# A tile table built in three parts, weights copied inside the last attention unit, and a routing exponential placed ahead of the first tile's silu

## The chip, the cores and the metric

One core of a Trainium2 chip runs the whole program. The metric is the device time of one execution in microseconds. The kernel before was timed three times: median 1210.19 us, from 1207.68 to 1212.79. One further execution was profiled; every row shown of the kernel before comes from it.

The engines are called PE (TensorE, with its weight loads apart as PEld), DVE (VectorE), ACT (ScalarE), POOL (GpSimd) and SP (SyncE, which here only issues transfers). Each runs its own list of instructions in order and waits at semaphores for the others.

## The reference

The input is 16 sequences of 512 tokens with 128 features. Two layers follow, each with a residual sum and a layer norm.

```
x = layernorm(x + attention(x))
x = layernorm(x + experts(x))
```

Attention has 16 heads of 8 features. Its softmax is taken twice over: half of the result is the usual softmax, half is the softmax without key 0, normalised again.

The expert layer routes every token to two of eight experts. The logits are x times gate_w; top 1 and top 2 are chosen, and each gets as its weight the softmax over those logits that lie within a jitter threshold of it:

```
mask1 = (m1 - logits) / maximum(abs(logits), m1) > 0.02
p1    = softmax(where(mask1, -inf, logits))     # weight of the first choice
mask2, p2 likewise for the second choice, the first one dropped
out  += wte[:, e] * ((silu(x @ w1[e].T) * (x @ w3[e].T)) @ w2[e].T)
```

All of this is computed in fp32 results, though scores are formed from bf16 parts.

## The kernel before

**Attention.** The work is cut into 64 units: a sequence (b, 0 to 15) and a group of four heads (g, 0 to 3). A loop over periods p runs on every engine, with eight steps k in each. In period p, PE forms the score products of unit p (two per step, 16 in all), ACT turns each into an exponential, and PE multiplies the exponentials of unit p - 1 with the values (four groups of eight matmuls, at the odd steps), which gather in one PSUM bank, acc_ps. DVE frees that bank by transposing it (`sums_by_query`), at step 0 of the period after. Score products pass through a ring of three PSUM banks, so PE can be at most three ahead of ACT. The row maxima of a unit are formed two periods ahead, so in the last two periods (62 and 63) there are none.

**Beside it.** While sequence b is attended to, the older ones are finished: normalised sums, output projection, layer norm (`ln_stats`, `ln_moments` on DVE, `inverse_deviation` on POOL, which also forms the logits), and the routing, 20 small DVE operations (`route(b, step)`) placed by the table ROUTE. Routing needs two results of ACT: `magnitudes` (absolute logits) and `routing_exp`, the exponential of the distances, which waits for the first eight steps. POOL's indirect transfers then scatter each token's row, twice, into the regions of its experts in rows_d.

**The tile table.** Rows of one expert are taken 256 at a time, as tiles. FIRST = 45 tiles are certain once 13 sequences are counted. `first_tables` on DVE, placed in period 62 at step 2, works out for each of them its expert, the first row in rows_d and the offset of its weights. It is a chain of small operations, each of which waits for the one before. Its parts are `whole_tiles`, `running_sum`, `tile_places` (expert of each tile, and the step within it), `tile_rows` (which ends with the semaphore s_tab_done) and `take` (how many tiles of each expert are used up).

**The expert tiles.** For each tile t, SP loads the rows by blocks (`load_blocks`, waits for s_tab_done) and once more whole (`load_rows`); DVE turns the blocks (`turn_rows`); ACT copies the expert's quarter of W1 and W3 out of the resident weights (`copy_weights`, two copies of 128x512, offsets read from the table); PE does `tile_up` (eight matmuls, L712), `tile_down` of the tile before (16 matmuls, L738), `tile_lin` (eight, L722); ACT the silu; DVE the product of both and the weighted result; POOL scatters the result into y_d. `tail(t)` on DVE and POOL, and a few lines on ACT, finish the last two sequences beside the first tiles. PE's values of the last unit (63) stand at t = 0 around the first tile, two groups ahead of `tile_lin(0)` and two behind. A last stage adds both results of each token to form the second layer norm.

**At the seam.** The order is written out by hand. Before its first tile, PE waits for the table, for all exponentials of the ring (s_ring_done, TAIL) and for all maxima. ACT waits, behind its last exponential, for the table, for W1 and W3, and copies the weights of tile 0, then of tile 1. DVE's list reads: the table (762 to 771 us), three routing steps of sequence 13, `sums_by_query(61)`, one more routing step, statistics, the turn of tile 0, `sums_by_query(62)`, nine routing steps of sequence 14. SP's list has, ahead of tile 4's blocks, the last quarter of W2 (`load_weights`, L470), which may go out once PE's last score product is done, since it overwrites keys and queries of attention. `tile_down(0)` waits for all of W2 (`pe.wait_ge(s_w2, 16 * NG)`).

Of the kernel before, what the change touches and what calls it, by code (L numbers as in the profile page):

```python
# [26 lines left out]
NB, L, D = 16, 512, 128  # L27
# [30 lines left out]
def layer(nc, xT, x, wqT, wkT, wvT, woT, bq, bk, bv, bo, gateT, w1T, w3T, w2T, out):  # L58
# [16 lines left out]
    with ctx:  # L75
# [501 lines left out]
        def _(pe):  # L577
# [146 lines left out]
                last.then_inc(s_lin, 1)  # L724

            def tile_down(t):
                if t == FIRST:
                    pe.wait_ge(s_tab_done, 3)
                expert = pe.value_load(woff_i[0:1, t:t + 1], min_val=0, max_val=(E - 1) * F)
                if t == 0:  # L730
                    pe.wait_ge(s_w2, 16 * NG)
                pe.wait_ge(s_h, t + 1)
                if t >= 2:
                    pe.wait_ge(s_y, t - 1)
                for w in range(halves(t)):
                    at = TK * (t % 2) + D * w
                    for c in range(FC):
                        last = nc.tensor.matmul(y_ps[:, at:at + D], HH[t % 2][:, c, P * w:P * (w + 1)],  # L738
                                                W2[:, bass.ds(expert + c * D, D)], start=(c == 0), stop=(c == FC - 1))
                last.then_inc(s_y_ready, 1)  # L740
# [5 lines left out]
                if (t, place) in TAIL_RING:  # L746
                    behind(*TAIL_RING[t, place])

            pe.wait_ge(s_tab_done, 1)
            pe.wait_ge(s_ring_done, TAIL)  # L750
            pe.wait_ge(s_mx_done, QC * UNITS)
            for t in range(TILES + 1):
                if is_tile(t):
# [24 lines left out]
        def _(act):  # L778
# [84 lines left out]
            def normed_rows(b, c):  # L863

                if c == 0:
                    act.wait_ge(s_rstd, 4 * (b + 1))
                nc.scalar.activation(XE[b % 2][:, c, 0, 0:D], ysum[:, c, :], ACT.Identity, scale=rstd[:, c:c + 1],
                                     bias=shift[:, c:c + 1]).then_inc(s_sent_step, 1)

            for p in PERIODS:  # L870
                b, g = divmod(p, NG)
                for k in range(STEPS):
                    if is_unit(p):
                        exp_chunk(p, 2 * k)
                        exp_chunk(p, 2 * k + 1)
                    if k == 1 and is_unit(p + 1):
                        negmax_rows(p + 1)
                    if (p, k) in ONCE:
                        behind(*ONCE[p, k])
                        if ONCE[p, k] == ("gw", 0):  # L880
                            for u in (0, 1):
                                load_first_queries(u)
                    if (g, k) in BEHIND:
                        name, off = BEHIND[g, k]
                        if is_seq(b + off):
                            behind(name, b + off)
                            if (name, b + off) == ("v1", 0):
                                for u in (2, 3):
                                    load_first_queries(u)
                    if g == 0 and k % 2 == 1 and is_seq(b - 2):  # L890
                        normed_rows(b - 2, k // 2)
                    if (g, k) == (0, 2) and is_seq(b - 2):
                        magnitudes(b - 2)
                    if (g, k) == (0, 6) and is_seq(b - 2):
                        routing_exp(b - 2)


            def copy_weights(t):
                if t >= 2:
                    act.wait_ge(s_lin, t - 1)  # L900
                if t == FIRST:
                    act.wait_ge(s_tab_done, 3)
                expert = act.value_load(woff_i[0:1, t:t + 1], min_val=0, max_val=(E - 1) * F)
                for to, held in ((W1T, W1), (W3T, W3)):

                    nc.scalar.activation(to[t % 2], held[:, bass.ds(expert, F)], ACT.Copy, scale=2.0)\  # L906
                      .then_inc(s_w_copied, 1)

            def small_tile_in(t):
                act.wait_ge(s_xgt_ready, t - FULL + 1)  # L910
# [1 line left out]
                nc.scalar.activation(XGT[t % 2][:, 0:n], xgt_ps[:, TK * (t % 2):TK * (t % 2) + n], ACT.Copy)\  # L912
                  .then_inc(s_xgt, 1)

            act.wait_ge(s_tab_done, 1)
            act.wait_ge(s_w13, 16 * 2 * NG)
            act.wait_ge(*split_done(NB - 1, 1))
            copy_weights(0)
            for t in range(TILES):
                if is_tile(t + 1):  # L920
                    copy_weights(t + 1)
                act.wait_ge(s_up, t + 1)
                if t == 0:
                    act.wait_ge(s_pv_ready, UNITS - 1)
                n = P * halves(t)
                nc.scalar.activation(SG[t % 2][:, :, 0:n], up_ps[:, :, 0:n], ACT.Silu).then_inc(s_silu, 1)  # L926
                if FULL <= t + 1 < TILES:
                    small_tile_in(t + 1)
                if t in (0, 10):
                    magnitudes(NB - 2 if t == 0 else NB - 1)  # L930
                if t in (2, 16):
                    for c in range(QC):
                        normed_rows(NB - 2 if t == 2 else NB - 1, c)
                if t in (1, 13):
                    routing_exp(NB - 2 if t == 1 else NB - 1)
                for place in range(2):
                    if (t, place) in TAIL_RING:
                        behind(*TAIL_RING[t, place])
# [12 lines left out]
        def _(dve):  # L951
# [180 lines left out]
            def tile_places(first, last):  # L1132
# [1 line left out]

                ge, gn = tile_by_expert(first, last)
                which = slice(first, last)
                no = tile_step[:, 0:last - first]

                def by_tile(x):
                    return x.unsqueeze(1).to_broadcast([1, last - first, E])  # L1140
# [4 lines left out]
                tb(V.tensor_tensor(ge, tile_no[:, 0:last - first].unsqueeze(2).to_broadcast([1, last - first, E]),  # L1145
                                   by_tile(cum), ALU.is_ge))
                tb(V.tensor_reduce(expert[:, which], ge, axis=AXX, op=ALU.add))
                tb(V.tensor_tensor(gn, ge, by_tile(move), ALU.mult))
                tb(V.tensor_reduce(no, gn, axis=AXX, op=ALU.add))

            def tile_rows(first, last, rows):
# [17 lines left out]
            def first_tables():  # L1169
# [7 lines left out]
                whole_tiles(cnt, TK)  # L1177
                running_sum()
                tile_places(0, FIRST)
                tile_rows(0, FIRST, TK)  # L1180
                take(FIRST)

            def full_by_expert():
                tb(V.tensor_tensor(cnt, offs[0:1, QC, :], eoff[0:1, :], ALU.subtract))
# [5 lines left out]
            def rest_by_expert():  # L1190
                tb(V.tensor_scalar_add(cnt, cnt, float(P - 1)))
                whole_tiles(cnt, P)
                tb(V.tensor_scalar(start, taken, float(HALVES), None, ALU.mult))
                tb(V.tensor_tensor(tiles, tiles, start, ALU.subtract))
                running_sum()

            for p in PERIODS:
                b, g = divmod(p, NG)
                for k in range(STEPS):
# [4 lines left out]
                    if is_seq(b - 1):  # L1204
# [8 lines left out]
                            ln_moments(b - 1, range(0, 1))  # L1213
                        elif (g, k) == (3, 4):
                            ln_moments(b - 1, range(1, 4))
                    if is_seq(b - 2) and (g, k) in ROUTE:
                        for step in ROUTE[g, k]:
                            route(b - 2, step)
                    if (g, k) == (3, 0) and is_seq(b - 1):
                        ln_stats(b - 1, range(0, 2))  # L1220
                    if (p, k) == (UNITS - 2, 2):
                        first_tables()


            def tail(t):
                if t == 0:
                    sums_by_query(UNITS - 2)
                    for step in range(0, 9):
                        route(NB - 2, step)
                elif t == 1:  # L1230
                    sums_by_query(UNITS - 1)
                    second_sums(NB - 1)
# [22 lines left out]
                    full_by_expert()  # L1255
                elif t == 24:
                    tile_places(FIRST, FULL)
                elif t == 26:
                    tile_rows(FIRST, FULL, TK)
                elif t == 28:  # L1260
                    take(FULL - FIRST)
                elif t == 30:
                    rest_by_expert()
                elif t == 32:
                    tile_places(FULL, TILES)
                elif t == 34:
                    tile_rows(FULL, TILES, P)

# [410 lines left out]
```

## Time and profile before

| | us |
|---|---|
| median of three runs | 1210.19 |
| profiled execution | 1210.04 |
| its span in the profile | 1208.3 |
| PE busy | 1129.0 (93%) |
| DVE busy | 918.8 (76%) |
| ACT busy | 831.2 (69%) |
| POOL busy | 660.6 (55%) |

Shares of busy time are means over three stages with different limits: attention (to about 786 us), tiles (to about 1160) and the last sums. The chain of waits gives PE 47% of the span and DVE 39%, of which the row maxima (L993) have 30%: they set the pace of attention, PE that of the tiles. The granted clock of PE has two levels here, 1.00 (2.4 GHz) and 0.50 (1.2 GHz); a value between them is a slice that holds both.

### The profile page before, as it was taken

Reading aid. Unit: us, or ns where it says so; the run is one execution under the profiler, and the core shown is the slowest. Engines: PE = TensorE matmul, PEld = TensorE weight load, DVE = VectorE, ACT = ScalarE, POOL = GpSimd, SP = SyncE. Lnnn points to the kernel's source line nnn. Section 1 sums busy time; section 2 is a strip of 40 time slices with the busy share of each in tenths; the row PEclk is TensorE's granted clock in tenths of the full one; section 3 lists DMA queues with packets and bytes.
Section 4 is the critical chain, followed back from the end, with each engine's and each line's share of the span. In section 5 each row is a group of like instructions: output and inputs, shape, how many; then the busy total and the mean of one; then the engine's idle time right before and its main releaser. Section 6 shows DMA issues by size and latency. Waiting matters only on the chain.

```text
span 1208.3 us, 23516 instructions
## 1 busy us (share of the span) xinstructions
PE 1129.0 (93%) x7114; PEld 564.7 (47%) x7117; DVE 918.8 (76%) x1328; ACT 831.2 (69%) x1691; POOL 660.6 (55%) x999
## 2 busy tenths in 40 slices
PE   4899999999999999999999998899999999999986
PEld 3322222222222222222222222169999999999952
DVE  6788999999999999999999999544545544443335
ACT  2278889889889889888888888654544443444636
POOL 4314546676676676676676654646545433333335
PEclk9889999999999999999999999789999999999999
DMA  5434344444444444444454454333434433321147
GB/s 163 138 94 123 104 117 129 119 132 127 121 133 126 122 131 125 121 135 122 123 135 115 123 148 150 90 75 80 93 74 103 90 78 74 79 64 40 42 162 265
DMA packets 170078, 138.46 MB, mean 115 GB/s; under 512 B 84564, under 2 KB 146648, under 8 KB 169953
## 3 DMA queue, kind: packets, MB, share of 16 engines
q1 hardware_dynamic: 160064, 117.22, 36.4%
q0 software_dynamic: 8688, 18.14, 4.5%
q10 hardware_dynamic: 1200, 1.57, 0.5%
q8 instruction: 60, 0.98, 0.4%
q14 instruction: 66, 0.53, 0.1%
HBM read 94.59 MB, written 42.19 MB: 113 GB/s over the span
## 4 chain that ended last, share of the span: by engine, by line
PE 47%; DVE 39%; issue 9%; DMA 2%; POOL 1%; ACTq 1%; SPq 1%; ACT 1%; POOLq 0%; DVEq 0%
DVE rowmax_sb L993 30%; PE ring_ps L738 10%; PE mx_ps L712 10%; PE mx_ps L722 10%; PE acc_ps L619 5%; PE ring_ps L607 5%; PE mx_ps L596 3%; DVE TN_sb L1002 3%; PE mx_ps L772 1%; PE ring_ps L652 1%; DVE stats_sb L1025 1%; DVE meanvar_sb L1032 1%; PE ring_ps L660 1%; DMA bo_sb<-bo 1%; DVE dist_sb L1060 0%
## 5 line engine op out<-in xcount | busy, mean ns | idle before, releaser
L794 ACT ACTIVATE probs_sb<-ring_ps 128x512 f32<-128x512 f32 x1024 | 558.2, 598 | 108.3 <-PE ring_ps L607 93.2
L993 DVE TENSOR_REDUCE rowmax_sb<-mx_ps 128x4 f32<-128x2048 f32 x256 | 585.8, 2288 | 32.3 <-PE mx_ps L596 26.8
L607 PE MATMUL ring_ps<-region_sb 74*128 74x512 bf16 x1024 | 315.9, 391 | 1.0 <-ACT probs_sb L794 0.9
L619 PE MATMUL acc_ps<-probs_sb,values_sb 128*32 128x512 f32 x2048 | 277.8, 616 | 4.1 <-DVE TN_sb L1002 4.1
L1628 POOL DMA_INDIRECT y_d<-probs_sb,values_sb x135 | 133.0, 985 | 206.4 <-DVE probs_sb L1293 182.3
L607 PEld LDWEIGHTS ring_ps<-region_sb 74*128 74x128 bf16 x1024 | 79.5, 97 | 321.3 <-ACT probs_sb L794 274.8
L906 ACT ACTIVATE xT_sb<-region_sb 128x512 f32 x78 | 49.1, 630 | 187.4 <-PE mx_ps L722 185.6
L1506 POOL DMA_INDIRECT rows_d<-sent_sb,pos_sb x128 | 130.2, 1017 | 41.0 <-issue 19.2
L1301 DVE TENSOR_TENSOR probs_sb<-mx_ps,probs_sb 128x1024 f32<-128x1024 f32 (+1 forms) x78 | 84.3, 1081 | 79.8 <-PE mx_ps L722 79.8
L596 PE MATMUL mx_ps<-k_maxima_sb,q_maxima_sb 32*128 32x512 bf16 x1024 | 101.9, 388 | 41.9 <-DVE rowmax_sb L993 41.5
L738 PE MATMUL ring_ps<-region_sb,probs_sb 128*128 x1080 | 135.8, 277 | 1.4 <-DVE probs_sb L1301 1.4
L1293 DVE SCALAR_TENSOR_TENSOR probs_sb<-ring_ps,values_sb 128x128 f32<-128x128 f32 x135 | 42.1, 347 | 121.1 <-issue 77.3
L712 PE MATMUL mx_ps<-k_parts_sb,xT_sb 128*128 128x256 f32 (+1 forms) x624 | 132.0, 355 | 1.9 <-ACT xT_sb L906 1.9
L738 PEld LDWEIGHTS ring_ps<-region_sb,probs_sb 128*128 128x128 f32 x1080 | 126.9, 191 | 12.5 <-issue 5.2
L712 PEld LDWEIGHTS mx_ps<-k_parts_sb,xT_sb 128*128 128x128 f32 x624 | 107.9, 192 | 15.2 <-issue 2.4
L619 PEld LDWEIGHTS acc_ps<-probs_sb,values_sb 128*32 128x32 f32 x2048 | 40.9, 109 | 103.9 <-issue 97.8
L596 PEld LDWEIGHTS mx_ps<-k_maxima_sb,q_maxima_sb 32*128 32x128 bf16 x1024 | 25.8, 91 | 115.0 <-DVE rowmax_sb L993 105.5
L926 ACT ACTIVATE probs_sb<-mx_ps 128x1024 f32<-128x1024 f32 (+1 forms) x78 | 70.5, 904 | 4.6 <-PE mx_ps L712 4.5
L722 PE MATMUL mx_ps<-k_parts_sb,full_q_sb 128*128 128x256 f32 (+1 forms) x312 | 65.6, 353 | 0.0
L722 PE MATMUL mx_ps<-k_parts_sb,full_k_sb 128*128 128x256 f32 (+1 forms) x312 | 64.6, 350 | 0.0
L1360 POOL CAST negmax_parts_sb<-negmax_sb 16x128 bf16<-16x128 f32 x64 | 17.9, 279 | 81.7 <-PE mx_ps L596 75.6
L722 PEld LDWEIGHTS mx_ps<-k_parts_sb,full_q_sb 128*128 128x128 f32 x312 | 51.6, 191 | 5.6 <-issue 1.1
(183 smaller groups left out, 1166.6 us busy)
## 6 DMA issues: line engine op xcount, KB each, us to landing
region_sb<-k_parts_d SPq DMA_DIRECT2D x64, 288.0 KB
region_sb<-q_parts_d SPq DMA_DIRECT2D x60, 288.0 KB
k_parts_d<-k_parts_sb SPq DMA_DIRECT2D x48, 256.0 KB, 2.5
k_maxima_sb<-k_parts_d SPq DMA_DIRECT2D x256, 32.0 KB
probs_sb<-y_d SPq DMA_DIRECT2D x32, 256.0 KB, 5.0
q_maxima_sb<-q_parts_d SPq DMA_DIRECT2D x244, 32.0 KB
values_sb<-rows_d SPq DMA_DIRECT2D x57, 132.0 KB, 2.2
q_parts_d<-q_parts_sb SPq DMA_DIRECT2D x16, 384.0 KB, 3.7
```

The costliest lines, as they stand in the source:

```text
L596: last = nc.tensor.matmul(mx_ps[:, j, :], q[rows, P * c:P * (c + 1)], k[rows, :], start=True, stop=True)
L607: nc.tensor.matmul(bank, KS[b % 2][0:KR + MR, h, P * c:P * (c + 1)], QS[b % 2][0:KR + MR, h, :], start=True, stop=True).then_inc(s_ring_re ...
L619: last = nc.tensor.matmul(acc_ps[VW * j:VW * (j + 1), 0, :], VE[b % 2][:, c, HG * g + j, :], PT[u % 2][:, j, c, :], start=(c == 0), stop=( ...
L712: last = nc.tensor.matmul(up_ps[:, c, 0:n], W1T[t % 2][:, P * c:P * (c + 1)], XGT[t % 2][:, 0:n], start=True, stop=True)
L722: last = nc.tensor.matmul(lin_ps[:, c, 0:n], W3T[t % 2][:, P * c:P * (c + 1)], XGT[t % 2][:, 0:n], start=True, stop=True)
L738: last = nc.tensor.matmul(y_ps[:, at:at + D], HH[t % 2][:, c, P * w:P * (w + 1)], W2[:, bass.ds(expert + c * D, D)], start=(c == 0), stop= ...
L794: nc.scalar.activation(PT[u % 2][:, i // QC, i % QC, :], ring_bank("st", u, i), ACT.Exp, scale=SCALE).then_inc(s_ring_done, 1)
L926: nc.scalar.activation(SG[t % 2][:, :, 0:n], up_ps[:, :, 0:n], ACT.Silu).then_inc(s_silu, 1)
L993: V.tensor_reduce(rowmax[u % 2][:, :].rearrange("p (j c) -> p j c", c=QC)[:, :, c], mx_ps[:, :, :], axis=AXX, op=ALU.max, negate=True).the ...
L1301: V.tensor_tensor(HH[t % 2][:, :, 0:n], lin_ps[:, :, 0:n], SG[t % 2][:, :, 0:n], ALU.mult)\
L1506: G.indirect_dma_start(rows_d, bass.IndirectOffsetOnAxis(ap=pos[b % 2][:, s, c:c + 1], axis=0), XE[b % 2][:, c, s, :], None).then_inc(s_sc ...
L1628: G.indirect_dma_start(y_d, bass.IndirectOffsetOnAxis(ap=XG[t % RING][:, w, D:D + 1].bitcast(i32), axis=0), YO[t % YRING][:, w, :], None, ...
```

## The change

DVE: `tile_places` loses its last two operations, which become `tile_steps`; `first_tables` ends after `tile_places`. `tile_steps` and `tile_rows` move to period 63, step 0, behind `sums_by_query(61)`. The routing steps 16 to 19 of sequence 13 (in periods 62, step 4, and 63, step 0) move to period 63, step 6, with `take` behind them. At the head of the tiles, routing steps 0 to 8 of sequence 14 change places with `sums_by_query(62)`.

ACT: the copies of tile 0's weights move, with their waits, into period 63 behind step 5, which is behind the twelfth of 16 exponentials. `magnitudes` and `routing_exp` of sequence 14 move from behind the silus of tiles 0 and 1 to ahead of the silu of tile 0.

PE: the waits for the table and for the ring's exponentials move from ahead of the first tile to the head of `tile_down(0)`.

```diff
@@ PE
             def tile_down(t):
+                if t == 0:
+                    pe.wait_ge(s_tab_done, 1)
+                    pe.wait_ge(s_ring_done, TAIL)
                 if t == FIRST:
...
-            pe.wait_ge(s_tab_done, 1)
-            pe.wait_ge(s_ring_done, TAIL)
             pe.wait_ge(s_mx_done, QC * UNITS)
@@ ACT (copy_weights itself is only defined earlier)
                     if (g, k) == (0, 6) and is_seq(b - 2):
                         routing_exp(b - 2)
+                    if (p, k) == (UNITS - 1, 5):
+                        act.wait_ge(s_tab_done, 1)
+                        act.wait_ge(s_w13, 16 * 2 * NG)
+                        act.wait_ge(*split_done(NB - 1, 1))
+                        copy_weights(0)
...
-            act.wait_ge(s_tab_done, 1)
-            act.wait_ge(s_w13, 16 * 2 * NG)
-            act.wait_ge(*split_done(NB - 1, 1))
-            copy_weights(0)
             for t in range(TILES):
                 if is_tile(t + 1):
                     copy_weights(t + 1)
+                if t == 0:
+                    magnitudes(NB - 2)
+                    routing_exp(NB - 2)
                 act.wait_ge(s_up, t + 1)
...
-                if t in (0, 10):
-                    magnitudes(NB - 2 if t == 0 else NB - 1)
+                if t == 10:
+                    magnitudes(NB - 1)
...
-                if t in (1, 13):
-                    routing_exp(NB - 2 if t == 1 else NB - 1)
+                if t == 13:
+                    routing_exp(NB - 1)
@@ DVE
                 tb(V.tensor_reduce(expert[:, which], ge, axis=AXX, op=ALU.add))
-                tb(V.tensor_tensor(gn, ge, by_tile(move), ALU.mult))
+
+            def tile_steps(first, last):
+                ge, gn = tile_by_expert(first, last)
+                no = tile_step[:, 0:last - first]
+                tb(V.tensor_tensor(gn, ge, move.unsqueeze(1).to_broadcast([1, last - first, E]), ALU.mult))
                 tb(V.tensor_reduce(no, gn, axis=AXX, op=ALU.add))
...
                 tile_places(0, FIRST)
-                tile_rows(0, FIRST, TK)
-                take(FIRST)
...
+            LAST_ROUTES = ((UNITS - 2, 4), (UNITS - 1, 0))
...
+                    if (p, k) == (UNITS - 1, 0):
+                        tile_steps(0, FIRST)
+                        tile_rows(0, FIRST, TK)
-                    if is_seq(b - 2) and (g, k) in ROUTE:
+                    if is_seq(b - 2) and (g, k) in ROUTE and (p, k) not in LAST_ROUTES:
                         for step in ROUTE[g, k]:
                             route(b - 2, step)
...
+                    if (p, k) == (UNITS - 1, 6):
+                        for at in LAST_ROUTES:
+                            for step in ROUTE[at[0] % NG, at[1]]:
+                                route(NB - 3, step)
+                        take(FIRST)
...
                 if t == 0:
-                    sums_by_query(UNITS - 2)
                     for step in range(0, 9):
                         route(NB - 2, step)
+                    sums_by_query(UNITS - 2)
```

The two later tables (at tiles 24 and 32) call `tile_steps` directly behind `tile_places`, so nothing changes there.

## Rows read from the trace of the kernel before

**Rows 1.** The page: granted clock of TensorE, in tenths, 40 slices of the span.
```profile
PEclk9889999999999999999999999789999999999999
```

**Rows 2.** Chain that ended last, at the seam: start us, us, what.
```profile
788.08 3.75 PE mx_ps L712 x8
...
794.83 1.93 PE mx_ps L722 x8
796.75 1.85 PE acc_ps L619 x16
798.60 1.93 PE mx_ps L712 x8
800.53 1.78 PE ring_ps L738 x16
```

**Rows 3.** Tiles: length, busy of PE PEld DVE ACT POOL, clock, DMA, GB/s.
```profile
900.00:1000.00 100.00, 100.00 (x611) 90.45 (x610) 51.28 (x129) 40.55 (x57) 45.47 (x47) 1.00 0.41 88
```

**Rows 4.** Timeline of PE: start, us, what, xcount, [idle before, releaser].
```profile
760.66 1.06 PE L619 MATMUL acc_ps<-probs_sb,values_sb 128*32 128x512 f32 x8
...
763.05 1.06 PE L619 MATMUL acc_ps<-probs_sb,values_sb 128*32 128x512 f32 x8
...
765.74 1.07 PE L619 MATMUL acc_ps<-probs_sb,values_sb 128*32 128x512 f32 x8
...
772.61 1.93 PE L619 MATMUL acc_ps<-probs_sb,values_sb 128*32 128x512 f32 x8 [4.12 <-DVE TN_sb L1002]
...
776.31 1.93 PE L619 MATMUL acc_ps<-probs_sb,values_sb 128*32 128x512 f32 x8
```

**Rows 5.** Stretches at the seam, columns as in rows 3.
```profile
770.00:771.00 1.00, 0.00 (x0) 0.00 (x0) 0.85 (x6) 0.00 (x0) 0.00 (x0) 0.61 0.26 74
794.00:796.00 2.00, 2.00 (x14) 1.12 (x7) 0.00 (x0) 0.00 (x0) 0.00 (x0) 0.97 0.33 70
```

**Rows 6.** Timeline of DVE at the seam, columns as in rows 4.
```profile
766.49 0.52 DVE L1147 TENSOR_REDUCE k_maxima_sb<-q_parts_sb 1x45 f32<-1x360 f32 x1
...
768.47 1.19 DVE L1155 TENSOR_TENSOR k_maxima_sb<-k_maxima_sb 1x45 f32<-1x45 f32 x1
...
770.55 0.17 DVE L1161 CAST k_maxima_sb<-k_maxima_sb 1x45 int32<-1x45 f32 x1
...
775.60 0.45 DVE L1275 STREAM_TRANSPOSE k_parts_sb<-q_maxima_sb 128x256 f32<-128x256 f32 x1 [1.16 <-DMA q_maxima_sb<-rows_d]
785.71 0.72 DVE L1002 STREAM_TRANSPOSE TN_sb<-acc_ps 128x512 f32<-128x512 f32 x1 [9.66 <-PE acc_ps L619]
...
786.75 1.98 DVE L1065 SCALAR_TENSOR_TENSOR absl_sb<-dist_sb,rev_sb 128x32 f32<-128x32 f32 x1
...
789.88 0.19 DVE L1065 SCALAR_TENSOR_TENSOR absl_sb<-dist_sb,rev_sb 128x32 f32<-128x32 f32 x1
```

**Rows 7.** Timeline of GpSimd (POOL) at the seam.
```profile
768.35 1.25 POOL L1451 TENSOR_TENSOR ysum_sb<-attn_out_sb,x_sb 128x512 f32<-128x512 f32 x1
774.52 0.20 POOL L1460 TENSOR_SCALAR rstd_sb<-meanvar_sb 128x4 f32<-128x4 f32 x1 [4.92 <-DVE meanvar_sb L1032]
...
787.39 1.28 POOL L1439 TENSOR_TENSOR x_sb<-x_sb,bo_sb 128x512 f32<-128x512 f32 x1
```

**Rows 8.** Timeline of ACT behind the last exponential.
```profile
786.22 0.60 ACT L794 ACTIVATE probs_sb<-ring_ps 128x512 f32<-128x512 f32 x1 [1.64 <-PE ring_ps L607]
787.30 0.63 ACT L906 ACTIVATE xT_sb<-region_sb 128x512 f32 x1 [0.49 <-issue]
...
789.51 1.28 ACT L926 ACT_TABLE_LOAD   x1
```

**Rows 9.** Timeline of SP; and landing of the weight load issued at 786.21.
```profile
783.85 0.40 SPq L530 DMA_DIRECT2D values_sb<-rows_d  x1
786.21 0.36 SPq L470 DMA_DIRECT2D region_sb<-w2T  x1
...
DMA to landing us min/median/max: 4.3/4.3/4.3
```

More of the change, by code:

```diff
@@ L868, in normed_rows, with copy_weights @@
                                      bias=shift[:, c:c + 1]).then_inc(s_sent_step, 1)
+            def copy_weights(t):
+                if t >= 2:
+                    act.wait_ge(s_lin, t - 1)
+                if t == FIRST:
+                    act.wait_ge(s_tab_done, 3)
+                expert = act.value_load(woff_i[0:1, t:t + 1], min_val=0, max_val=(E - 1) * F)
+                for to, held in ((W1T, W1), (W3T, W3)):
+                    nc.scalar.activation(to[t % 2], held[:, bass.ds(expert, F)], ACT.Copy, scale=2.0)\
+                      .then_inc(s_w_copied, 1)
             for p in PERIODS:
@@ L895, in _ @@
                         routing_exp(b - 2)
[L898 to L907, printed above, removed]
+                    if (p, k) == (UNITS - 1, 5):
[3 more added lines that the diff above has]
+                        copy_weights(0)
             def small_tile_in(t):
@@ L1136, in tile_places @@
                 which = slice(first, last)
-                no = tile_step[:, 0:last - first]
                 def by_tile(x):
@@ L1257, in tail @@
                     tile_places(FIRST, FULL)
+                    tile_steps(FIRST, FULL)
                 elif t == 26:
@@ L1265, in tail @@
                     tile_places(FULL, TILES)
+                    tile_steps(FULL, TILES)
                 elif t == 34:
```

## The prediction

> **What bounds the kernel now.** I read the page's clock line first: TensorE (PE) has its full clock in all but two places, and one slice near four fifths of the run stands at 7 [rows 1]. That slice is the seam between attention and the expert tiles. The chain of waits there goes through VectorE (DVE), PE, ScalarE (ACT) and PE again; from the first tile on it is PE alone, tile after tile [rows 2]. Table by stretch: PE is busy 100.00 of 100 us between 900 and 1000 [rows 3], 611 matmuls at 32 a tile, so 5.24 us a tile with no gap. What makes the first tile's down product start earlier therefore ends the run as much earlier, as long as transfers keep up.
>
> In the seam the timeline of PE shows the loss. The last attention unit but one runs at a pace of 763.05 - 760.66 = 2.39 us per pair of steps [rows 4]. Then PE idles 4.12 us (768.49 to 772.61) for the transposition that frees acc_ps, which stands on DVE behind the whole tile table. In this idle time the granted clock falls: 0.61 in the slice from 770 to 771 [rows 5], where PE had been idle since 768.49. Afterwards a pair takes 776.31 - 772.61 = 3.70 us [rows 4], and the first tile's up product 3.75 us where the same eight matmuls take 1.93 once the clock is back at about 794 [rows 2, 5].
>
> **The change part by part, on the profiled execution** (1210.04 us, its span 1208.3; the median of the runs shown is 1210.19, 0.15 above, which I neglect).
>
> *Table in three parts.* The first part now ends with the reduce of L1147, at 766.49 + 0.52 = 767.01 [rows 6]. The transposition of unit 61's sums follows at once, because its input was done at 765.74 + 1.07 = 766.81 [rows 4]. It takes 0.72 [rows 6], so the bank is free at about 767.8, before 768.49 when PE wants it. The 4.12 us go. If a DVE operation were held up as L1155 was (1.19 us instead of some 0.2), 0.4 us would come back; I take 0.
>
> *The table itself.* L1148 and L1149 come behind the transposition, some 0.7 us later than before; L1154 and L1155 then fall into GpSimd's residual sum of 1.25 us at 768.35 [rows 7], as L1155 did before (768.47 to 769.66). That held-up time swallows most of the 0.7: the table is ready at about 770.9 instead of 770.72 [rows 6]. SyncE (SP) starts its loads 0.2 us later; bounds 0 and 0.7. Nothing in unit 63's first half waits for the table any more.
>
> *Deferred routing of sequence 13 and "take".* They leave the place ahead of the moments and come behind them. GpSimd's deviation work was released by the moments at 774.52 [rows 7], 3.80 us after the table; without the take (four operations), three routing steps and the transposition in between it comes some 1.5 us earlier, and the four routing steps (under 1 us) run beside its first operations, ahead of the logits that wait for them. No cost; at worst 0.5 us on logits that have slack until the first tile's rows have landed and been turned at 775.60 + 0.45 [rows 6].
>
> *Unit 63.* At full clock its four groups of values start at about 768.5, 770.9, 773.3 and 775.7.
>
> *Weights copied behind the twelfth exponential.* Before, the copies came after the last exponential with a gap of 0.49, and four took 789.51 - 787.30 = 2.21 [rows 8], 0.55 each. Two cost ACT 0.49 + 1.10 = 1.6 us. PE meanwhile has one score product and the last values to do (1.06), so its last score product, which without copies would come at 775.7 + 1.06 = 776.7, waits for the thirteenth exponential: the twelfth ends at about 775.4, 1.6 for the copies and 0.60 more [rows 8] make 777.6, so 1.0 us is lost and the product starts at 777.7. Bounds: 0 if the three ring banks cover it all, 2.2 if nothing does. The table has been ready for 4 us by then, and SP issues the last loads of W1 and W3 in unit 60's period.
>
> *PE's waits moved into the first down product.* The first up product no longer waits for the last exponentials, only for turned rows (776.3) and copied weights (777.0): it starts at about 777.9 instead of 788.08. At full clock up, values, lin, values take 1.93 + 1.85 + 1.93 + 1.85 = 7.56 [rows 2], so up(1) starts at 785.5 and down(0) could start at 787.4, against 800.53: 13.1 us earlier.
>
> *Magnitudes and routing exponential ahead of the first silu; routing ahead of the transposition on DVE.* Behind the turn at 776.05 (+0.2) come nine routing steps. They took from 786.4, the end of the transposition, to 789.88 + 0.19 = 790.1, and one was held for 1.98 instead of some 0.2 [rows 6]; so 1.9 us without, 3.7 with: done at 778.2, or 780.0. Then the transposition of unit 62: 778.9 or 780.7. PE wants it after up(0), at 779.8, so it costs 0 to 0.9 us. On ACT: last exponential done at 777.6 + 3 x 0.60 = 779.4, two copies 1.6, magnitudes and exponential 0.5 (an estimate: the unheld routing steps of the same rows take 0.2 each on DVE), function load 1.28 [rows 8], silu 1.0 (an estimate: half of the 2.21 that four 128x512 copies took): done at 783.9, wanted by up(1) at 785.5. Hidden, with 1.6 us of cover; queued behind it on ACT are only later copies. Two later function loads go, beside a busy PE: nothing.
>
> *What is late next: the last quarter of W2.* SP's order is unchanged and it has no wait to lose: its row load for tile 1 was issued at 783.85 and ended at 784.25; only the weights behind it waited, until 786.21, for PE's last scores [rows 9]. These now come first, so the weights go out at about 784.5 and land 4.3 us later (what this transfer took), at 788.8. down(0) waits for them: 788.9 instead of 800.53. So of PE's 13.1 us, 1.5 us are given back, and the same 1.5 us hide small delays upstream (the DVE holding above, half of the uncertainty of the copies). Sum: 800.53 - 788.9 = 11.6 us earlier, 1210.04 - 11.6 = 1198.4 us. Later block and row loads come in the order and at the spacing of before, where PE never waited for them between 900 and 1000 [rows 3].
>
> **A rule against it.** In units 62 and 63 PE works through three ring banks with short idle times, and the trace keeps the full clock there until the long idle time begins [rows 4, 5]. The Trainium skill ("TensorE: Matmul & The Clock Gate", section "A second HAM failure mode: psum-queue depth-cycling") says that frequent micro-idles between matmul groups that cycle through PSUM banks can make the clock fall and rise again. No run here shows it for unit 63 without the 4.12 us; by that rule the first rival below would hold, by the row the forecast.
>
> **The rivals.**
> *The clock falls anyway,* at the 1.0 us for the copies or at the short waits around. For: the fall came 1.9 us into an idle time. Against: unit 62 held the clock. Price: if it falls at the copies, PE is fully busy from 777.9, and before, the clock came back at 794.3, 6.2 us after such work began at 788.08; 6.2 us at half clock lose 3.1, of which W2 hides 1.5: 1200.0. If it falls in the first half of unit 63, four pairs lose 1.3 each besides: 1205.2. Middle 1202.
> *The held-up DVE or the ACT order becomes the wait.* Two holdings of 1.75 us in the nine steps put the end of the transposition at 778.2 + 3.5 + 0.7 = 782.4, 2.6 after PE wants it: less the 1.5 that W2 hides, 1.1 us are lost, 1199.5; with first blocks landing 2 us later besides, 1201.5. For: GpSimd has eight scatters in this time. Against: the step held before ended with GpSimd's add of 1.28 us at 787.39 [rows 7], and that add now comes behind the scatters, after the nine steps.
> *It doesn't free PE:* the first part of the table still ends after 768.49 + 1.9, and the clock falls as before. Then the idle time is shorter by about 2 us and the copies overlap: 1205 to 1206. Against: the stretch up to L1147 is unchanged code with unchanged neighbours.
> *Slower:* the clock falls in unit 63 and the wait for W2 and for the first tiles' blocks breaks PE's work up again, so that it stays low into the tiles. Each tile at half clock costs 5.24 us more; from 11.6 / 5.24 = 2.2 tiles on the gain is gone, and with four tiles low the time is 1210.04 - 11.6 + 21.0 = 1219.4. Against: before, the clock rose before the second tile began, with worse gaps.
>
> **How the numbers follow.** Forecast 0.66 (1196.5 to 1200.5: W2 a little earlier or later, runs differing by some 2 us); clock falls 0.17 (1200 to 1205.2); DVE or ACT order 0.09 (1199.5 to 1201.5); PE not freed 0.05 (1205.5); slower 0.03 (1219.4). If W2 came without any wait the time would be 1196.9; a run 2 us low makes 1194.9. Range 1195 to 1204. About 0.5% (6 us, so below 1204.1 and above 1216.2) can be told from no change: faster 0.91, same 0.06, slower 0.03.
>
> **What would show it.** Right: in unit 63 no idle time of PE before L619, granted clock 1.00 through the seam, about 2.4 us a pair; two copies on ACT between exponentials; the first up product near 778, PE waiting 1 to 2 us in front of the first down product with W2's transfer as releaser; the first tile's silu before up(1); then tiles at 5.24 us. Wrong: half clock in any slice from 768 to 790, PE waiting for the transposition or ACT for the routing steps, or the first down product after 792.

## Result: 0.72% faster, by the seam as predicted, with a smaller gain in the medians than in the profile

| | us |
|---|---|
| before, median of 6 runs | 1208.76 (1206.94 to 1212.79) |
| changed, median of 6 runs | 1200.62 (1200.21 to 1201.15) |
| ratio, 95% interval | 0.9928 (0.9916 to 0.994) |
| predicted | 1198.4, range 1195 to 1204 |
| profiled execution changed | 1200.69, span 1199.0 |
| profiled execution before | 1210.04, span 1208.3 |

Three of the six runs of the kernel before are those whose median stands in its section on the time. The medians differ by 8.1 us, the two profiled executions by 9.35; the sum of the prediction was 11.6.

The page's clock line of the changed kernel has no 7 at the seam any more [rows 1]; the 8 at the right end lies behind the last product, the one near the left in the start, where nothing changed.

```profile
PEclk9989999999999999999999999999999999999998
```

The chain that ended last, changed kernel: it no longer comes from DVE's table through ACT's copies. It runs through SP's list of loads to the transfer of W2, and from there along PE [rows 2].

```profile
785.30 0.40 SPq L530
...
785.74 4.41 DMA region_sb<-w2T
...
790.28 2.05 PE ring_ps L741 x16
```

Timeline of PE, changed kernel (start, us, what, count, idle before and its releaser). The values of unit 62 follow without idle time at 2.4 us a group (769.43, 771.83, and so on to 776.62, where [rows 4] had 4.12 us of idle time and then 3.70 a group); the last score product waits 0.59 us for the copies; the first up product starts at 778.50 and takes 1.89, not 3.75. Then PE waits 2.33 us for W2.

```profile
766.74 1.07 PE L619 MATMUL acc_ps<-probs_sb,values_sb 128*32 128x512 f32 x8
...
769.43 1.07 PE L619 MATMUL acc_ps<-probs_sb,values_sb 128*32 128x512 f32 x8
...
771.83 1.07 PE L619 MATMUL acc_ps<-probs_sb,values_sb 128*32 128x512 f32 x8
...
776.62 1.06 PE L619 MATMUL acc_ps<-probs_sb,values_sb 128*32 128x512 f32 x8
778.28 0.39 PE L607 MATMUL ring_ps<-region_sb 74*128 74x512 bf16 x1 [0.59 <-ACT probs_sb L795]
778.50 1.89 PE L712 MATMUL mx_ps<-k_parts_sb,xT_sb 128*128 128x256 f32 x8
...
785.96 1.99 PE L712 MATMUL mx_ps<-k_parts_sb,xT_sb 128*128 128x256 f32 x8
790.28 2.05 PE L741 MATMUL ring_ps<-region_sb,probs_sb 128*128 x16 [2.33 <-DMA region_sb<-w2T]
```

The granted clock of four stretches over the seam, columns as in rows 3: 1.00 throughout, also over the 2.33 us of waiting (786 to 792), against [rows 5].

```profile
768.00:774.00 6.00, 5.48 (x32) 1.54 (x30) 5.15 (x20) 5.17 (x11) 1.64 (x3) 1.00 0.49 144
774.00:780.00 6.00, 5.15 (x29) 2.18 (x29) 3.61 (x19) 5.33 (x11) 4.67 (x9) 1.00 0.38 58
780.00:786.00 6.00, 6.00 (x43) 2.32 (x41) 1.99 (x4) 4.43 (x8) 4.47 (x6) 1.00 0.57 125
786.00:792.00 6.00, 3.67 (x27) 3.12 (x24) 3.01 (x7) 1.02 (x1) 2.14 (x2) 1.00 0.72 180
```

Timeline of DVE, changed kernel: the first part of the table ends at 767.46 + 0.52, the transposition follows 0.32 us later, the table is complete at 771.95 + 0.17. L1162 took 0.82 us instead of 0.29, while GpSimd's sum ran (769.50 to 770.77), as L1155 did before [rows 6, 7]. None of the nine routing steps behind the turn was held: the transposition follows at 779.38.

```profile
767.46 0.52 DVE L1151 TENSOR_REDUCE k_maxima_sb<-q_parts_sb 1x45 f32<-1x360 f32 x1
768.30 0.72 DVE L1007 STREAM_TRANSPOSE TN_sb<-acc_ps 128x512 f32<-128x512 f32 x1 [0.32 <-DVE k_maxima_sb L1151]
...
770.01 0.82 DVE L1162 TENSOR_TENSOR k_maxima_sb<-tile_no_sb,k_maxima_sb 1x45 f32<-1x45 f32 x1
...
771.95 0.17 DVE L1169 CAST k_maxima_sb<-k_maxima_sb 1x45 int32<-1x45 f32 x1
...
779.27 0.19 DVE L1070 SCALAR_TENSOR_TENSOR absl_sb<-dist_sb,rev_sb 128x32 f32<-128x32 f32 x1
779.38 0.71 DVE L1007 STREAM_TRANSPOSE TN_sb<-acc_ps 128x512 f32<-128x512 f32 x1
```

Timeline of ACT, changed kernel (L795 exponentials, L879 copies): two copies between exponentials, two behind the last, one function load of 1.28 us, the silu from 782.29, which up(1) wants at 785.96.

```profile
776.59 0.63 ACT L879 ACTIVATE xT_sb<-region_sb 128x512 f32 x1 [0.34 <-issue]
...
777.64 2.04 ACT L795 ACTIVATE probs_sb<-ring_ps 128x512 f32<-128x512 f32 x4
779.55 0.65 ACT L879 ACTIVATE xT_sb<-region_sb 128x512 f32 x1
...
780.71 0.27 ACT L862 ACTIVATE expd_sb<-dist_sb 128x64 f32<-128x64 f32 x1
781.00 1.28 ACT L931 ACT_TABLE_LOAD   x1
782.29 1.02 ACT L931 ACTIVATE probs_sb<-mx_ps 128x1024 f32<-128x1024 f32 x1
```

GpSimd's deviation work was released at 773.99, and this is the row that answers to 774.52 in [rows 7].

```profile
773.99 0.20 POOL L1478 TENSOR_SCALAR rstd_sb<-meanvar_sb 128x4 f32<-128x4 f32 x1 [3.22 <-DVE meanvar_sb L1037]
```

In comparing times within the seam one thing must be known: the attention stage of this execution was already late by about 1.0 us when the seam began (unit 61's last values at 766.74 against 765.74 in [rows 4]), though nothing differs up to there. Some 0.9 us of the lateness arise in the first 75 us (the first transposition of acc_ps starts at 76.27 against 75.39), and other executions differ by as much. Below, the length of the seam is therefore counted from the start of those values to the first down product: 800.37 - 765.74 = 34.6 us before, 790.28 - 766.74 = 23.5 us changed. By the prediction's numbers it was 788.9 - 765.74 = 23.2.

### The profile page after: what moved, and what is told of

The parts are those of the page before. It is cut to its first block, busy times and chain, and to the rows that moved or that the text cites. A ratio compares the mean times of both kernels' runs of the same rounds, so it can differ in the third digit from the quotient of the medians.

```text
span 1199.0 us, 23515 instructions
## 1 busy us (share of the span) xinstructions
PE 1121.4 (94%) x7114; PEld 563.5 (47%) x7117; DVE 917.7 (77%) x1328; ACT 828.0 (69%) x1689; POOL 660.1 (55%) x999
## 4 chain that ended last, share of the span: by engine, by line
PE 46%; DVE 39%; issue 9%; DMA 2%; SPq 2%; POOL 1%; ACTq 1%; ACT 0%; POOLq 0%; DVEq 0%
DVE rowmax_sb L998 31%; PE ring_ps L741 10%; PE mx_ps L722 10%; PE mx_ps L712 9%; PE ring_ps L607 5%; PE acc_ps L619 4%; PE mx_ps L596 3%; DVE TN_sb L1007 3%; PE mx_ps L773 2%; PE ring_ps L652 1%; DVE stats_sb L1030 1%; DVE meanvar_sb L1037 1%; PE ring_ps L660 1%; DMA bo_sb<-bo 1%; SPq L522 1%
## 5 line engine op out<-in xcount | busy, mean ns | idle before, releaser
L795 ACT ACTIVATE probs_sb<-ring_ps 128x512 f32<-128x512 f32 x1024 | 558.1, 598 | 99.2 <-PE ring_ps L607 83.9
L619 PE MATMUL acc_ps<-probs_sb,values_sb 128*32 128x512 f32 x2048 | 273.2, 606 | 0.0
L879 ACT ACTIVATE xT_sb<-region_sb 128x512 f32 x78 | 49.2, 630 | 186.2 <-PE mx_ps L722 184.8
```

Of the source, the lines that this page charges most:

```text
L619: last = nc.tensor.matmul(acc_ps[VW * j:VW * (j + 1), 0, :], VE[b % 2][:, c, HG * g + j, :], PT[u % 2][:, j, c, :], start=(c == 0), stop=( ...
L795: nc.scalar.activation(PT[u % 2][:, i // QC, i % QC, :], ring_bank("st", u, i), ACT.Exp, scale=SCALE).then_inc(s_ring_done, 1)
```

## Experiments

Theory: the seam lost twice, by PE's idle time behind the table and by the half clock that the idle time brings on; and in the changed kernel the last transfer of W2 stands in the way of the rest. Rivals: the clock falls whatever PE does; the copies and ACT's order carry the gain; the tiles give the lead back.

| run | edit | median us (runs) | ratio to before, 95% | seam us | low clock at the seam |
|---|---|---|---|---|---|
| before | | 1208.76 (6) | | 34.6 | 770.2 to 794.1 |
| changed | | 1200.62 (6) | 0.9928 (0.9916 to 0.994) | 23.5 | none |
| e1 | changed, W2 early | 1196.97 (6) | 0.9902 (0.9883 to 0.9922) | 21.0 | none |
| e2 | before, idle filled | 1204.01 (12) | 0.9963 (0.9952 to 0.9974) | 26.4 | none |
| e3 | table split alone | 1200.87 (6) | 0.9941 (0.9918 to 0.9964) | 24.2 | none |
| e4 | all but the split | 1206.11 (12) | 0.9979 (0.9965 to 0.9993) | 30.2 | 770.6 to 787.6 |
| e5 | e1, copies late | 1199.44 (6) | 0.9925 (0.9906 to 0.9945) | 24.2 | 780.0 to 783.4 |
| e6 | e1, exponential late | 1196.56 (6) | 0.9903 (0.9884 to 0.9922) | 21.0 | none |
| changed again | | 1201.16 (6) | 0.9938 (0.9919 to 0.9958) | 23.5 | none |
| e7 | e1, one copy inside | 1196.35 (6) | 0.9893 (0.9868 to 0.9917) | 20.8 | none |
| e8 | e5, idle filled | 1199.61 (6) | 0.9926 (0.99 to 0.9952) | 22.5 | none |

The low stretch is worked out from the granted clock of slices: 0.61 in a slice of 1 us is 1.00 for 0.22 us of it and 0.50 for the rest. Seams and low stretches are those of one profiled execution each. Each ratio from e1 on is taken against runs of the kernel before made beside that experiment, with medians of 1208.49 (e1 to e4), 1209.07 (e5, e6 and changed again) and 1209.05 (e7, e8).

**e1: W2 ahead of tile 2's blocks.**

```diff
-                if t == BRING:
+                if t == 2:
                     load_weights(UNITS - 1, s_w2, (W2, w2T))
```

> The changed kernel with the last quarter of W2 issued two tiles earlier in SP's list (ahead of tile 2's blocks, not tile 4's). Theory (after the change the transfer of W2 is what is late: PE waits 2.33 us for it in front of the first down product): it lands near 783.5, PE's wait goes, and the time falls by 2.0 to 2.4 us, to about 1198.4. Rival 1 (the first blocks, pushed back by 0.5 us, or the product on DVE become late instead): PE waits elsewhere, 1199.5 to 1201. Rival 2 (the tiles give the lead back because SP or POOL set their pace): 1200.6, with new idle times of PE among the tiles.

Timeline of PE, e1: no waiting in front of the first down product.

```profile
787.00 1.95 PE L741 MATMUL ring_ps<-region_sb,probs_sb 128*128 x16
```

Measured 1196.97, 3.65 us under the changed kernel where 2.0 to 2.4 were expected. The seam is 2.5 us shorter, which is the wait, and neither rival shows in the trace: W2 is issued at 777.9 and lands 3.9 us later, from the first tile's up product on PE waits for nothing up to 800 us, and the first twelve tiles take 64.7 us as in the changed kernel (64.8). So the theory on W2 holds. The rest of the gain is not the seam. From the same late down product to the end e1 took 112.2 us (from 1083.04), the changed kernel 112.6 in its first profile (1086.42 to 1199.0) and 113.4 in a second one (1085.51 to 1198.9), with the same code; and the first came 0.8 us later to its seam than e1. These are single executions; why the medians differ by 1.2 us more than the seams stays open.

**e2: the idle time filled.**

```diff
+                    if (p, k) == (UNITS - 1, 1):
+                        pe.wait_ge(s_mx_done, QC * UNITS)
+                        for n in range(18):
+                            nc.tensor.matmul(mx_ps[:, 0, :], KS[1][:, 0, 0:P], KS[1][:, 0, :], start=True, stop=True)
                     if k % 2 == 1 and is_unit(p - 1):
                         values(p - 1, c)
```

> The kernel before with 18 matmuls of 128x512 bf16 without use (into the banks of the row maxima, idle by then) put on PE ahead of the values that wait for the table; everything waits as before, but PE is busy meanwhile (18 x 0.216 = 3.9 of the 4.12 us). Theory (the seam loses twice: the idle time itself, and the half clock that follows it): the clock stays at 1.00, a pair of steps takes 2.4 instead of 3.70 us, the first products 1.8 instead of 3.75, and the time falls by 6 to 7 us against the kernel before, to about 1202.3, though the table is as late as ever. Rival (the clock falls in unit 63 whatever PE does, for its micro-idles): no gain, 1208 to 1209.

Timeline of PE, e2: the values come as late as ever, but from there the groups stand 2.4 us apart.

```profile
773.06 1.06 PE L619 MATMUL acc_ps<-probs_sb,values_sb 128*32 128x512 f32 x8
...
775.46 1.06 PE L619 MATMUL acc_ps<-probs_sb,values_sb 128*32 128x512 f32 x8
...
783.43 1.97 PE L716 MATMUL mx_ps<-k_parts_sb,xT_sb 128*128 128x256 f32 x8 [1.79 <-ACT xT_sb L910]
...
792.79 1.95 PE L742 MATMUL ring_ps<-region_sb,probs_sb 128*128 x16
```

Stretches of e2 over the seam:

```profile
768.00:774.00 6.00, 5.86 (x30) 2.05 (x29) 5.45 (x23) 2.13 (x5) 1.55 (x2) 1.00 0.49 139
774.00:784.00 10.00, 7.43 (x44) 2.04 (x41) 3.51 (x16) 8.14 (x16) 7.08 (x11) 1.00 0.44 85
```

The clock was 1.00 throughout, so the fall belongs to the idle time and not to the micro-idles (the idle times of some 0.3 us between products) of the unit. The seam is 8.2 us shorter than in the first profile of before, but the medians differ by 4.5 us, not by 6 to 7: the first sign that the first profile stands for the longer cases.

**e3 and e4: either half alone.** e3 takes the DVE half only, the table in three parts and the deferred routing (the code of the kernel before on ACT and PE, and `sums_by_query(62)` ahead of the routing steps); e4 puts the table in one piece again and the routing back:

```diff
                 tile_places(0, FIRST)
+                tile_steps(0, FIRST)
+                tile_rows(0, FIRST, TK)
+                take(FIRST)
...
-                    if (p, k) == (UNITS - 1, 0):
-                        tile_steps(0, FIRST)
-                        tile_rows(0, FIRST, TK)
...
-                    if (p, k) == (UNITS - 1, 6):
...
```

> The DVE half of the change alone: table in three parts and deferred routing; weights copied, PE's waits, routing exponential and the order of the transposition as in the kernel before. Theory (W2 hides what the other half saves): first up product about 1.5 us later than in the changed kernel, PE ready for the first down product near W2's landing; 1200.6 to 1201.6, so nearly all of the gain. Rival (PE idles over 2 us for the copies, the clock falls there): 1203 to 1205.

> The ACT and PE half alone: the table in one piece in period 62 again, the rest as changed. Theory (the idle time and the fall of the clock come back, and only the copies overlap): 4.1 us idle, 0.50 clock from 770, the first up product some 2 us earlier than in the kernel before, 1206.5 to 1207.5. Rival (the copies and the order of ACT carry a good part of the gain): 1203 to 1205.

Timeline of PE, e3: 1.89 us for the copies, 1.55 for W2.

```profile
779.13 1.97 PE L712 MATMUL mx_ps<-k_parts_sb,xT_sb 128*128 128x256 f32 x8 [1.89 <-ACT xT_sb L878]
...
790.21 2.05 PE L738 MATMUL ring_ps<-region_sb,probs_sb 128*128 x16 [1.55 <-DMA region_sb<-w2T]
```

Timeline of PE and one stretch, e4: the idle time and the half clock are back.

```profile
772.66 1.94 PE L619 MATMUL acc_ps<-probs_sb,values_sb 128*32 128x512 f32 x8 [3.95 <-DVE TN_sb L1007]
...
776.37 1.93 PE L619 MATMUL acc_ps<-probs_sb,values_sb 128*32 128x512 f32 x8
...
796.12 1.95 PE L741 MATMUL ring_ps<-region_sb,probs_sb 128*128 x16
```

```profile
772.00:786.00 14.00, 13.34 (x45) 2.29 (x46) 4.67 (x21) 7.19 (x14) 8.87 (x13) 0.50 0.48 90
```

The split alone gave 1200.87, the whole change 1200.62 and 1201.16: the other half adds nothing that the medians can show, with one run of e3 at 1204.94. In the traces it brings the first up product 1.4 us forward, counted within the seam, and shortens the seam by 0.7 (24.2 to 23.5); the rest goes into a longer wait for W2 (1.55 to 2.33 us). The other half alone (e4) gave 2.4 us. Both theories held, e4 with 0.4 us more gain than expected; its profiled execution had 17 us of low clock where the first profile of before had 23.9.

**e5 and e6: the two parts of the other half, with W2 out of the way.** e5 is e1 with the copies and PE's waits as in the kernel before, e6 is e1 with the exponential, the magnitudes and the transposition as before.

> W2 issued early as in e1, and the weight copies and PE's waits as in the kernel before (copies behind the last exponential); table split and routing exponential as changed. With W2 out of the way this shows what the copies are worth. Theory (copies behind the last exponential delay the first up product by 1.4 us, as the traces of e3 and e1 have it: 779.13 against 777.72): 1198.4, against 1197.0 of e1, with PE idle 1.9 us ahead of the first tile and the clock kept. Rival (that idle time lets the clock fall): 1199.5 to 1202, with 0.50 in the slices behind it.

> W2 issued early as in e1, and the routing exponential, the magnitudes and the order of the transposition on DVE as in the kernel before; the rest as changed. Theory (this part of the change moved only hidden work): the same as e1 within 0.5 us, 1196.5 to 1197.5, with two function loads more on ACT beside a busy PE. Rival (the two loads, 2.6 us, push a silu past PE's need of it): 1198 to 1199.6, with PE waiting for ACT in the first three tiles.

Timeline of PE and stretches, e5: PE idles 1.89 us for the copies, and here the clock falls, at about 780.0 (1.3 us behind the end of that idle time), for 3.4 us. In e3, with the same idle time of 1.89 us, it did not fall.

```profile
778.68 2.47 PE L712 MATMUL mx_ps<-k_parts_sb,xT_sb 128*128 128x256 f32 x8 [1.89 <-ACT xT_sb L878]
781.08 3.05 PE L619 MATMUL acc_ps<-probs_sb,values_sb 128*32 128x512 f32 x16
```

```profile
780.00:782.00 2.00, 2.00 (x11) 0.63 (x14) 0.00 (x0) 1.97 (x5) 1.53 (x2) 0.50 0.74 174
782.00:784.00 2.00, 2.00 (x16) 0.33 (x8) 0.00 (x0) 0.69 (x1) 1.55 (x2) 0.65 0.71 167
```

The rival had its place: 1199.44, 2.5 us over e1 where 1.4 were expected, and the profiled execution shows why it can be more: its seam is 3.1 us longer than that of e1. Timeline of PE, e6:

```profile
786.33 1.95 PE L741 MATMUL ring_ps<-region_sb,probs_sb 128*128 x16
```

e6 is level with e1 (1196.56, the same seam of 21.0), so the exponential ahead of the silu was worth nothing here, as the prediction had it.

**The changed kernel again.**

> The changed kernel once more, beside the experiments on the same chip. Theory (its profiled attention started 0.9 us late by chance; W2 costs 2.3 to 2.5 us of e1's 3.65 us): 1199.4 to 1200.7, the wait for W2 again between 2.1 and 2.6 us. Rival (e1 gains more than the wait): 1200.6 and a wait of 2.3 us with other idle time that e1 lacks.

1201.16 and a seam of 23.5 us again, with 2.27 us of waiting for W2; its attention was 0.9 us earlier than in the first profile. Its median is 0.5 above what was expected, and its six runs spread over 3.3 us (1199.09 to 1202.36), so the 0.94 us of the first six understate how much it varies. The rival is not out: e1's median lies 4.2 us under this one, with a seam only 2.5 us shorter. In the two profiles, 3.7 us apart, the rest is 1.2 us in the last sums, with the same code; no idle time that e1 lacks was found among the tiles.

**Three more profiles of the kernel before.**

> The kernel before, one more look at its seam. Theory (how long the clock stays low behind the 4.1 us idle time differs between executions, so one profile mis-sizes it): a low stretch of another length than the 23.9 us of the first profile, and a time that differs by about half of that difference in busy time. Rival (the low stretch is fixed by the program): 23.9 us again.

> The kernel before, a third look at its seam. Theory (the length of the low clock differs between executions): a low stretch other than the 23.9 us that both looks so far have. Rival (fixed by the program): 23.9 us a third time.

> The kernel before, a fourth look, for the same question as the third: low stretch other than 23.9 us by the one theory, 23.9 us by the other.

The second profile agrees with the rival: low clock for 23.9 us again. The third and the fourth don't. Stretches of the third, then of the fourth profile:

```profile
772.00:774.00 2.00, 1.03 (x8) 0.16 (x8) 1.86 (x9) 0.00 (x0) 0.00 (x0) 0.96 0.53 126
774.00:790.00 16.00, 14.25 (x47) 3.95 (x44) 5.18 (x16) 10.04 (x18) 11.25 (x15) 0.50 0.54 121
790.00:792.00 2.00, 2.00 (x15) 0.78 (x18) 0.00 (x0) 1.04 (x2) 0.00 (x0) 0.78 0.44 92
```

```profile
770.00:772.00 2.00, 0.25 (x4) 0.18 (x8) 1.86 (x10) 0.00 (x0) 0.00 (x0) 0.96 0.49 133
772.00:774.00 2.00, 2.00 (x10) 0.14 (x3) 1.30 (x7) 0.00 (x0) 0.25 (x2) 0.50 0.40 56
774.00:776.00 2.00, 2.00 (x12) 0.41 (x10) 0.45 (x1) 1.76 (x4) 1.83 (x5) 0.69 0.31 46
776.00:790.00 14.00, 11.64 (x74) 4.66 (x73) 3.44 (x12) 9.85 (x18) 9.18 (x10) 1.00 0.61 142
```

Low from 773.8 to 790.9 (17 us) in the third, from 771.8 to 775.2 (3.4 us) in the fourth. Timeline of PE, fourth profile: one group of values at half clock, the rest at full.

```profile
771.75 1.91 PE L619 MATMUL acc_ps<-probs_sb,values_sb 128*32 128x512 f32 x8 [3.68 <-DVE TN_sb L1002]
...
775.37 1.06 PE L619 MATMUL acc_ps<-probs_sb,values_sb 128*32 128x512 f32 x8
...
792.75 1.95 PE L738 MATMUL ring_ps<-region_sb,probs_sb 128*128 x16
```

Their seams are 34.7, 32.0 and 27.4 us, and their times 1209.64, 1208.40 and 1202.64. Against the 26.4 us of e2, whose table comes as late but whose clock stays full, the same program loses between 1 and 8 us by the clock at one idle time of 3.7 to 4.1 us. What decides how long the clock stays low these runs do not show.

**e7 and e8.** e7 is e1 with only W1's copy behind the twelfth exponential:

```diff
-                        copy_weights(0)
+                        copy_weights(0, slice(0, 1))
...
+            copy_weights(0, slice(1, 2))
             for t in range(TILES):
```

e8 is e5 with eight useless matmuls ahead of PE's waits for the first tile.

> e1 (W2 early) with only the copy of W1's tile inside the last unit; that of W3, which the first lin product wants 3.6 us later, goes behind the last exponential. Theory (two copies hold up the last score product by about 0.6 us, one copy by none): PE's 0.59 us in front of its last score product goes, 1196.2 to 1196.7 against 1197.0 of e1. Rival (ACT's chain copy, copy, copy, exponential, function load, silu becomes late for the second tile's up product): 1197 to 1198.

> e5 (W2 early, copies behind the last exponential) with 8 matmuls of 128x512 bf16 without use on PE in the 1.9 us in which it waits for the copies. Theory (in e5 that idle time lets the clock fall in some executions, which makes its times spread): no 0.50 at the seam, 1198.0 to 1198.8, a spread under 2 us where e5 had 3.7. Rival (e5's spread and its excess over e1 have another cause): 1199.4 and the same spread.

Timeline of PE, e7, and then e8:

```profile
777.11 1.89 PE L712 MATMUL mx_ps<-k_parts_sb,xT_sb 128*128 128x256 f32 x8
...
786.62 1.95 PE L741 MATMUL ring_ps<-region_sb,probs_sb 128*128 x16
```

```profile
778.59 1.97 PE L712 MATMUL mx_ps<-k_parts_sb,xT_sb 128*128 128x256 f32 x8
```

In e7 the 0.59 us went, and the up product follows the last scores. But PE then waits 0.15 us for a transposition behind that product, and of the gain 0.3 us are left at the first down product (a seam of 20.8 against 21.0). 1196.35 is the lowest median of all (0.9893 of before), as expected, but within the spread of e1 and e6, so the medians do not show this gain. e8 missed: its profiled execution had the full clock and took 1198.65, but three of its six runs took 1200.6 to 1201.8, a spread of 3.4 us where e5 had 3.7, and its median is level with e5's. That is what the rival said. In the profiled executions the fall of the clock costs e5 1.7 us of its seam (24.2 against 22.5), but the medians do not show it; what makes the longer runs of both long stays open.

## Why the prediction was right, and where its size was off

Times of the changed kernel are given here less the 1.0 us by which its attention was late.

- **Table in three parts:** right. No idle time ahead of the values, full clock. Predicted 768.5 for the first values, 768.4 found; the table ready at 770.9 predicted, 771.1 found.
- **Deferred routing:** right; GpSimd's deviation work 1.5 us earlier as worked out, no cost.
- **Copies inside the unit:** 1.0 us of delay predicted for the last score product, 0.59 found: the gap ahead of the copies was 0.34 and not 0.49, the twelfth exponential ended 0.15 earlier than worked out, and the thirteenth began 0.1 ahead of the second copy's end. First up product at 777.9 predicted, 777.5 found.
- **ACT's order:** hidden as predicted, with 2.7 us of cover (1.6 predicted). No routing step was held.
- **W2:** this was the step that set the end, as predicted. Down product at 788.9 predicted, 789.3 found: the load went out 0.2 later (the table) and landed in 4.41 us, not 4.3. e1 shows the wait by itself.
- **The tiles:** predicted to carry the lead through in full. Of the lead at the first down product 0.5 us are lost in the first twelve tiles (from the first to the thirteenth down product 64.8 us, before 64.3). The trace shows one 0.49 us gap of PE's weight loads in front of tile 8's down product with no releaser, which lengthens that tile by 0.25 us, half of the loss; the same gap stands in e3. The loss goes with the DVE half: every run that has it, e3 too, takes 64.7 to 64.9 us over these tiles, and every run without it (e2, e4 and all four profiles of the kernel before) 64.3 to 64.4. By what way the DVE half, or the shorter seam that it brings, causes the loss is open.
- **The rule weighed against it** ("TensorE: Matmul & The Clock Gate", section "A second HAM failure mode: psum-queue depth-cycling", of the Trainium skill): in unit 63 PE had idle times of 0.26, 0.26, 0.26 and 0.59 us between products through the ring (in e7 without the last one), and the granted clock stayed at 1.00 in both profiles and in e1, e6 and e7. Here the measurement decides against it.

Where the sum was off: "the median of the runs shown is 1210.19, 0.15 above, which I neglect". That was the mis-sized term. For the seam the prediction was within 0.4 us: 800.37 - 788.9 = 11.5 us shorter predicted, 34.6 - 23.5 = 11.1 found. (The 11.6 of its sum has the first down product at 800.53, as the chain shows it; the timeline has 800.37.) But the profiled execution of before had a low clock of 23.9 us, as long as in any of four profiles (23.9, 23.9, 17, 3.4). The kernel before takes 1202.3 to 1212.8 over its runs. In the last three profiles the time follows the seam (34.7, 32.0 and 27.4 us; 1209.64, 1208.40 and 1202.64), so the price of the idle time, different each time, accounts for much of this spread; for the runs without a profile that is inferred. The change took this price out, 1 to 8 us, and filling the idle time alone gave 4.5 us in the medians (e2). From the profiled pair the gain is 34.6 - 23.5 = 11.1, less 1.0 (start of attention), 0.5 (tiles) and 0.3 (last sums) = 9.3 us, the difference found. In the medians it is 8.1, since that of before lies 1.3 us under its profiled execution.

The time alone would not have told the forecast from its rivals: 1200.62 lies just outside the forecast's own band (1196.5 to 1200.5) and inside those of two rivals, the falling clock (from 1200) and the order on DVE and ACT (1199.5 to 1201.5). The traces decide: the clock stayed at 1.00, no routing step was held, and PE's one long wait was for W2. One reading of the prediction was off without changing its sum: the clock fell 1.7 us into the idle time (0.61 in the slice from 770 puts the fall at 770.2), not 1.9. Nor is that a fixed delay: in the second profile of before the fall came 1.9 us into the idle time, in the third and the fourth 0.9 and 0.1 us behind its end.

## What to carry to other kernels

A chain of small operations on an engine with time to spare is free only until a buffer has to be freed from behind it: cut it where the busy engine's next need falls, not where it fits. When a wait on the path is removed, look at once for the next transfer in the list whose place was set by the old wait: moving W2's load two tiles earlier shortened the seam by another 2.5 us. And where an idle time of PE brings on the half clock, one profile does not price it: take several before writing the sum.

## What was not expected of the hardware

The same idle time of about 4 us before the same matmuls was followed by 3.4, 17 or 24 us at 1.2 GHz in four executions. An idle time of 1.89 us was followed by 3.4 us at half clock in e5 and by none in e3, and one of 2.33 us (the changed kernel) by none, so the length of the idle time alone does not decide.

Switching from the exponential to the silu cost ACT the 1.28 us of the load and nothing more that the trace shows: the load began 0.02 us behind the operation before it (780.71 + 0.27) and the silu 0.01 us behind its end. The Trainium skill ("ScalarE: Activation LUTs", section "What ACT_TABLE_LOAD costs") adds a drain of about 1.38 us to each switch; here the trace has no room for it.
